# Two transformer layers on one core: a reordered routing chain, A.V in 32-column quarters in both layers, and identity products between the layers

## What is computed

```
x = x + tanh(g_xattn[0]) * L0_xattn(layernorm(x), ctx, ctx, mask)      # masked
x = x + tanh(g_ffn[0])   * L0_ffn(layernorm(x))                        # top-1 of 8 experts, 128 -> 512 -> 128, gelu
x = x + tanh(g_xattn[1]) * L1_xattn(layernorm(x), ctx, ctx)            # no mask
x = x + tanh(g_ffn[1])   * L1_ffn(layernorm(x))                        # top-2 of 16 experts, 8 slots each and batch
```

## Time and profile before

| | us |
|---|---|
| median of 3 runs | 534.26 (531.89 to 535.05) |
| the profiled execution's own time | 535.57 |
| its span, first to last instruction | 533.60 |
| layer 0 attention alone (TensorE all but uninterrupted) | about 17 to 184 |
| first experts | about 186 to 281 |
| layer 1 attention | about 289 to 440 |
| second experts, with the end of layer 1 | about 437 to 533 |

### The profile page before, as it was taken

One profiled execution on the slowest core, in us unless ns is written; L12 is line 12 of the kernel. 1 busy time (PEld: TensorE's weight loads), 2 busy tenths in 40 slices (PEclk: granted clock), 3 DMA queues, 4 the chain that ended last, 5 costly groups with the idle time before them and its releaser, 6 DMA issues.

```text
span 533.6 us, 19576 instructions
## 1 busy us (share of the span) xinstructions
PE 452.7 (85%) x7243; PEld 337.8 (63%) x7243; DVE 365.5 (68%) x977; ACT 322.0 (60%) x764; POOL 273.5 (51%) x325
## 2 busy tenths in 40 slices
PE   2789999998988896999985789988898777778887
PEld 1456776776776695999982466665565556444454
DVE  5678777978686857355542779889998786553455
ACT  2355565565765684677744566767667556775553
POOL 2522533556553347888886535353535316533455
PEclk9999999999999989799996799999999997899999
DMA  7114343232101134665445010110031000000112
GB/s 200 49 53 140 80 117 110 72 106 75 43 12 52 30 80 119 80 97 77 49 38 149 1 44 5 42 32 24 3 92 31 16 2 3 1 1 12 34 46 71
DMA packets 50620, 30.53 MB, mean 57 GB/s; under 512 B 12384, under 2 KB 46944, under 8 KB 50528
## 3 DMA queue, kind: packets, MB, share of 16 engines
q1 hardware_dynamic: 37072, 18.54, 12.9%
q0 software_dynamic: 6640, 4.67, 6.6%
q10 hardware_dynamic: 6816, 6.07, 4.0%
HBM read 19.41 MB, written 9.85 MB: 55 GB/s over the span
## 4 chain that ended last, share of the span: by engine, by line
PE 54%; DVE 14%; issue 13%; POOL 8%; ACT 6%; DMA 3%; ACTq 1%; DVEq 1%; SPq 0%; POOLq 0%
PE T_ps L861 8%; PE A_ps L876 7%; PE S_ps L850 7%; POOL x_mid L1140 6%; DVE maxes L603 5%; PE S_ps L844 3%; PE m_H_ps L1427 3%; PE Q_ps L831 2%; PE f_H_ps L1192 2%; PE m_T_ps L1467 2%; PE Q_ps L752 2%; PE m_X_ps L1454 2%; PE m_X_ps L1410 2%; PE X_ps L893 2%; PE Q_ps L763 2%
## 5 line engine op out<-in xcount | busy, mean ns | idle before, releaser
L603 DVE TENSOR_REDUCE maxes<-S_ps 128x8 f32<-128x512 f32 x128 | 87.6, 684 | 45.7 <-PE S_ps L850 45.6
L430 POOL TENSOR_TENSOR k_blk<-kT,col_a 128x512 f32<-128x512 f32 x64 | 67.7, 1068 | 86.2 <-ACT kT L491 59.7
L533 ACT ACTIVATE probT<-T_ps 128x512 f32<-128x512 f32 x128 | 76.0, 594 | 43.3 <-PE T_ps L861 42.8
L611 DVE TENSOR_TENSOR prob<-S_ps,maxes 128x512 f32<-128x512 f32 x128 | 88.5, 692 | 4.4
L861 PE MATMUL T_ps<-col_a,prob 128*128 128x128 f32 x512 | 83.2, 286 | 9.8 <-DVE prob L611 6.8
L861 PEld LDWEIGHTS T_ps<-col_a,prob 128*128 128x128 f32 x512 | 56.8, 143 | 47.1 <-issue 34.7
L1140 POOL DMA_INDIRECT x_mid<-f_out,f_rows x39 | 60.9, 1561 | 12.1 <-issue 10.7
L876 PEld LDWEIGHTS A_ps<-v_blk,probT 128*32 128x32 f32 (+1 forms) x3072 | 53.0, 119 | 10.6 <-issue 10.4
L876 PE MATMUL A_ps<-v_blk,probT 128*32 128x18 f32 (+1 forms) x3072 | 59.3, 195 | 0.0
L850 PE MATMUL S_ps<-k_blk,qT 32*64 32x256 f32 x1024 | 46.2, 415 | 5.4 <-DVE prob L611 2.9
L1005 DVE TENSOR_TENSOR f_hid<-f_H_ps,f_b 128x512 f32<-128x512 f32 x39 | 27.0, 692 | 33.3 <-PE f_Y_ps L1206 28.5
(11 more groups left out here) (198 smaller groups left out, 876.3 us busy)
## 6 DMA issues: line engine op xcount, KB each, us to landing
f_w<-in_W ACTq DMA_DIRECT2D x16, 256.0 KB, 2.8
ctxT<-in_ctxT SPq DMA_DIRECT2D x12, 256.0 KB, 3.1
f_rows<-sorted_rows SPq DMA_DIRECT2D x39, 64.5 KB, 2.0
out<-m_final SPq DMA_DIRECT2D x32, 64.0 KB, 1.5
x_all<-in_x SPq DMA_DIRECT2D x6, 256.0 KB, 5.0
x_mid<-x_all SPq DMA_DIRECT2D x6, 256.0 KB, 3.1
x_all<-x_mid SPq DMA_DIRECT2D x6, 256.0 KB, 3.7
ctxT<-in_ctxT SPq DMA_DIRECT2D x8, 128.0 KB, 2.6
```

The source lines that it names most:

```text
L430: nc.gpsimd.tensor_tensor(k_blk[:, t % 2, :, :, :], kT[:, g.at(R), t - g.first, :].rearrange("p (b k) -> p b k", b=2).unsqueeze(2).to_broa ...
L533: nc.scalar.activation(probT[:, t % 2, 4 * h:4 * h + 4, :], T_ps[:, :, :], ACT.Exp, scale=SCALE).then_inc(probT_ready, 1)
L603: nc.vector.tensor_reduce(maxes[:, t % 2, h, :, :], half_of(h), X, ALU.max).then_inc(max_ready, 1)
L611: nc.vector.tensor_tensor(prob[:, t % 2, heads, :].rearrange("p (r e) k -> p r e k", r=2), half_of(h), maxes[:, t % 2, h, :, :].unsqueeze( ...
```

## The change

1. **Ranks first.** `rank`/`rank_slots` move in TensorE's list from behind the last `logit` to directly behind the second half of `turn_probs`, ahead of `attend`; `keep_ranks` moves in ScalarE's list from behind `q_out` to directly behind the second `exp`. The times `when` stay.
2. **Single scatters.** In layer 0 the scatters of the groups 0 to 4 are laid one a step, where they were two a step.
3. **Quarters in layer 0 too.** `attend` and `logit` take 32-column parts in both layers.
4. **Identity products.** Matmuls of the identity with itself, whose results nobody reads and which wait for nothing. Five of 512 columns (`stream`) go into `tensor_ahead`, one behind each of its three `project_k` and two `project_v`, and three more (`STREAMED`) behind the last. Three (`awake`) go into layer 1's first steps, into T_ps: 256 columns behind the first `turn_x` (time 28.05), 256 behind the first `project_q` (30.01), 512 ahead of the first `turn_probs` (31).

```diff
--- before.py
+++ after.py
@@ -100,6 +100,7 @@
 EXPERTS_AT = MOVES_AT + NT // 8
 RAISE_AT = EXPERTS_AT + 5
 SINGLY = 7
+STREAMED = 3
 F1_PARTS = 4
 F1_FROM = NT + 19
 ONE_BY_ONE = GROUPS[SINGLY].first
@@ -476,7 +477,7 @@
             blocks = gpsimd_steps(pool)
             steps = [(blocks, tiles if masked else tiles[2:], shift(-2)), (norm, groups, head(-10)), (r_norm, groups, settled(3, 6, short, later))]
             if masked:
-                steps += [(scatter, tiles, lambda t: settled(8 if GROUP_OF[t].own < 7 else 7, 13, short, later)(GROUP_OF[t]) + (t - GROUP_OF[t].first) // 2)]
+                steps += [(scatter, tiles, lambda t: settled(8 if GROUP_OF[t].own < 7 else 7, 13, short, later)(GROUP_OF[t]) + (t - GROUP_OF[t].first) // (1 if GROUP_OF[t].own < LAST_GROUPS else 2))]
             else:
                 steps += [(gaps, groups, settled(7, 11, short, later))]
             steps += [(add_bias, groups, head(-4))]
@@ -587,8 +588,8 @@
                                          accum_out=r["total"][:, t:t + 1]).then_inc(raised_done, 1)
 
             k_out, v_out = scalar_steps(act)
-            steps = [(exp(1), tiles, shift(0)), (keep_logits, groups, settled(6, 9, short, later)), (avT_out, groups, tail(2)), (q_out, groups, head(-2)),
-                     (keep_ranks, groups, settled(7 if masked else 8, 12, short, later)), (v_out, late_units, unit_head(-1)), (k_out, late, head(-3)),
+            steps = [(exp(1), tiles, shift(0)), (keep_ranks, groups, settled(7 if masked else 8, 12, short, later)), (keep_logits, groups, settled(6, 9, short, later)), (avT_out, groups, tail(2)), (q_out, groups, head(-2)),
+                     (v_out, late_units, unit_head(-1)), (k_out, late, head(-3)),
                      (exp(0), tiles, shift(-1)), (r_xnT_out, groups, settled(5, 8, short, later)), (xnT_out, groups, turn_x_at), (normed, tiles, normed_at), (r_normed, units, lambda u: settled(4, 7, short, later)(u.group))]
             if not masked:
                 steps += [(raise_, groups[:SINGLY], tail(12)), (raise_last, [None], lambda _: RAISE_AT)]
@@ -766,9 +767,18 @@
 
             return project_k, project_v
 
+        def stream_into(bank, n):
+            eye = w["ident"][:, :]
+            nc.tensor.matmul(bank[:, 0:n, :], eye, eye.unsqueeze(1).to_broadcast([P, n, P]), start=True, stop=True)
+
         def tensor_ahead(pe):
             project_k, project_v = tensor_steps(pe, x_banks["q"])
-            return [(project_k, early, k_ahead), (project_v, early_units, v_ahead)]
+
+            def stream(_):
+                stream_into(S_ps[1][:, 0, :].rearrange("p (u k) -> p u k", k=P), Q)
+
+            return [(project_k, early, k_ahead), (stream, early, k_ahead), (project_v, early_units, v_ahead), (stream, early_units, v_ahead),
+                    (stream, range(STREAMED), lambda n: 2 * NT)]
 
         def tensor(pe):
             ident = w["ident"]
@@ -797,7 +807,7 @@
             def logit(g):
                 pe.wait_ge(r_xnT_ready, g.i + 1)
                 router_bank(g).take(logits_read, g.i + 1)
-                part = P if masked else QUARTER
+                part = QUARTER
                 for u in range(g.n):
                     for c in range(P // part):
                         rows = slice(c * part, (c + 1) * part)
@@ -869,7 +879,7 @@
                 pe.wait_ge(v_ready, u.i + 1)
                 wait(pe, divided, u.i)
                 pe.wait_ge(probT_ready, 2 * t + 2)
-                part = S if masked else QUARTER
+                part = QUARTER
                 for j in range(HP):
                     for c in range(P // part):
                         queries = slice(c * part, (c + 1) * part)
@@ -894,10 +904,13 @@
                 last.then_inc(y_made, 1)
 
             score_ahead = (score, tiles, score_at)
-            steps = [score_ahead, (turn_probs(1), tiles, shift(0)), (attend, tiles, shift(1)), (logit, groups[:7], settled(6, 9, short, later)),
+            awake = [] if masked else [(lambda n: stream_into(T_ps, n), [Q // 2], lambda _, when=when: when) for when in (NT - 3.95, NT - 1.99)]
+            awake += [] if masked else [(lambda n: stream_into(T_ps, n), [Q], lambda _: NT - 1)]
+            steps = [score_ahead] + awake + [(turn_probs(1), tiles, shift(0)),
+                     (rank if masked else rank_slots, groups, settled(7 if masked else 8, 12, short, later)), (attend, tiles, shift(1)), (logit, groups[:7], settled(6, 9, short, later)),
                      (turn_av, groups, tail(2)), (project_q, groups, head(-2)), (output, groups, tail(3)),
                      (logit, groups[7:], settled(6, 9, short, later)),
-                     (rank if masked else rank_slots, groups, settled(7 if masked else 8, 12, short, later)), (project_v, late_units, unit_head(-1)), (project_k, late, head(-3)),
+                     (project_v, late_units, unit_head(-1)), (project_k, late, head(-3)),
                      (turn_probs(0), tiles, shift(-1)), (turn_r, groups, settled(5, 8, short, later)), (turn_x, groups, turn_x_at)]
             run(hook["first_tensor"](pe) + steps + hook["tensor"](pe))
```

## The result

The kernel after takes 530.01 us (median of 9 runs, 528.1 to 534.7), the kernel before 534.26 (531.89 to 537.29); beside each other on one chip the ratio is 0.9908, 95% interval 0.9881 to 0.9934. The direction was forecast, the size was not: 9.9 us were expected, 4.3 to 5 came. The profiled execution took 529.13 (span 527.0), that of before 535.57: 6.4 apart.

The account below looks back on a forecast made before the run. TensorE was taken to bound layer 0, VectorE's need near. Terms 6.9 + 0.9 + 0.4 + 0.5 + 1.2 + 0.7 = 10.6, less 0.7 for new waits, give 9.9 us: from 534.26 to 524.3, range 520.5 to 528.5.

Parts of the forecast that it names:

- the loop's minimum: Layer 0: scores wait for the previous tile's subtractions, so no interval between tiles' first maxima falls much below 4.27 us.
- Rival A: VectorE or the new rank waits take most of the gain; layer 0 gives 3 us, total 530.5; chance 0.18.
- Rival B: All room in the intervals is used: 14.8 us in layer 0, 17.8 in all, total 516.5; chance 0.11.
- Rival C: TensorE's clock falls inside layer 0 because A.V is shorter; at eight tiles 15 us, total 539; chance 0.05.
- 1.2 together: Layer 1: bank waits removed by ranks first, in intervals with room 0.77, 0.65 and 0.26, give 1.2 us.
- 0.7 of it goes: Second experts: ScalarE's 1.02 us wait before keeping ranks, ahead of a normalization the experts' moves need, shrinks by 0.7 us.
- waits for the one-hot: Both layers: rank moved ahead waits for `choose` without A.V as cover; cost 0 to 5.7 us, taken as 0.7.
- Scatters, put at 0: Layer 0: single scatters only spread 16 scatters of about 1.0 us; gain 0, at most 1 either way.
- the term of layer 0: Savings summed interval by interval over layer 0, each capped by TensorE's room there: 6.9 us, ends 3 to 14.8.
- The handoff and the drain: Layer 0's end to the first up-product gains 0.9 us; one logit group in the first experts gains 0.4.
- Between the layers: Identity products keep TensorE's clock up; nothing before layer 1's first maximum, 0.5 us from the scores and products behind.
- Rival D: Identity products get in the way, the clock falls at 284 anyway; 6.4 us gained, total 527.9; chance 0.10.

Follow-up runs that it names:

- the first two sets: Kernel before with one part of the change each; then the whole, quarters again, and the whole less ranks or less identity products; ratios to before 0.9863 to 0.9998.
- only_ranks: Kernel before with only rank and keep_ranks moved ahead; ratio 0.9987 (0.9955 to 1.002).
- only_scatters: Kernel before with only single scatters in groups 0 to 4 of layer 0; ratio 0.9991 (0.9965 to 1.0016).
- row_reduced: Kernel after without VectorE's cast of the row numbers, the sum before it writing the integers itself; ratios to the kernel before 0.9933 and 0.9934.

## Why the prediction was wrong

**What held.** TensorE bounds layer 0, and quarters are the change: 187 ns for 212, the loop's minimum still 4.27, the stretch of the experts unchanged. Of the intervals, 2, 7, 10, 18, 22, 23 and 28 gave 0.26, 0.38, 0.38, 0.30, 1.16, 0.42 and 0.98, where 0.37, 0.37, 0.37, 0.30, 1.28, 0.37 and 0.91 stood; 24 and 27 gave nothing, as said. Rival A had the time nearly right (530.5) and in part for the right reason: the ranks of layer 1 give nothing; but VectorE's own need didn't cap layer 0 at 3. Rival B fell: layer 0 gave 5.8, not 14.8. Rival C was right that the clock falls inside layer 0, and wrong in the size: it stayed at 1.00 in the profiled execution, but fell in all seven other traces of the first two sets whose kernels change layer 0, for up to 1.9 us an interval, in one to three intervals, where C needed six to eight tiles. C's reason, the shorter A.V, is not shown: only_ranks and only_scatters leave A.V as it was and have a fall too. That the kernel after was profiled in an execution without a fall is luck.

**The step that failed: the ranks.** "1.2 together" for layer 1 and "0.7 of it goes" for the second experts. The prediction did price waits for the one-hot, at 0.7 of a possible 5.7, on the ground that they fall where TensorE idles for VectorE. It did not set them against the removed waits one by one. Side by side they are 5.10 and 5.56 us. From tile 37 to 58, where the 1.2 stood, the kernel takes 93.3 us with the edit and 93.4 without, and the ratio of the whole without it, 0.9909, can't be told from 0.9900. In layer 0 the ranks gave some 1.0 us in one pair of traces, half of it by where a held operation falls. In 14 and 22 the room is shared: ranks alone shorten them to 4.59 and 4.50, quarters alone to 4.71 and 4.31, both to 4.63 and 4.39. At the second experts nothing was seen to come back either: the rank that ScalarE kept after 1.02 us of waiting is now kept at once,

```profile
436.76 0.28 ACT L572 COPY rank_now<-Q_ps 128x128 f32<-128x128 f32 x1
```

and the stretch behind tile 58 is 1.0 us longer all the same, at a lower clock (0.88 for 0.92), so the 0.7 was not seen and is not disproved. The two terms are 1.9 us of the 9.9.

**Intervals that lengthened.** 11, 14 and 17 gave 0.58, 0.81 and -0.38 for 0.80, 1.17 and 0.72; 26 gave -0.67 for 0.19, and 3, to which nothing was assigned, gave -0.76. 3 and 26 are the held operations. The intervals that the prediction named gave 4.2 of their 6.9 us. Others, put at 0, gave 1.6: 15, 19, 21 and 25 came out 1.15, 0.38, 0.48 and 0.54 shorter, 3 and 29 0.76 and 0.21 longer. In 15, 19, 21 and 25 VectorE had no wait for scores in the row that ends the interval, so its filled time was read as its own need; in 15 and 19 that filled time held operations of `choose` that took 1.02, 0.97 and 0.94 us and could shorten. In 17 TensorE stood in the middle of the logits, now 32 short products where there were eight, with no wait that the profile shows. The logits in quarters alone lengthened it as well, to 5.90 and 5.91 us, and A.V alone shortened it to 4.93, so the stop comes with the quarters of the logits:

```profile
101.90 0.42 PE L814 MATMUL X_ps<-col_b,r_xnT 128*32 128x8 f32 x29
...
103.55 0.23 PE L814 MATMUL X_ps<-col_b,r_xnT 128*32 128x8 f32 x3 [1.22 <-issue]
```

**Scatters, put at 0.** From tile 1 to 20 the kernel before takes 95.4 us, scatters alone 93.9, quarters alone 94.0, the whole 92.3. So the trace of the kernel after holds some 1.5 us that the prediction had put down to nothing. Most of it comes from interval 15: before, two operations of `choose` took 1.02 and 0.97 beside two `k_blk` in a row (0.17 to 0.19 each elsewhere), with single scatters they lie apart and take 0.17 and 0.18. (Behind tile 20 single scatters shift time: alone they make 25 shorter by 0.53 us and 26 longer by 0.54.) Without this the term of layer 0, 6.9, would have come out near 4.3. In the times the scatters alone are not to be told from 0.

**The handoff and the drain**, 0.9 and 0.4, gave 0.5 and -0.1. **Between the layers** the products did hold the clock up to tile 32, and 0.5 was to come from the scores behind. There it fell after all, in a wait for VectorE:

```profile
289.93 0.66 PE L871 MATMUL T_ps<-col_a,prob 128*128 128x128 f32 x4 [2.50 <-DVE prob L612]
291.34 1.16 PE L860 MATMUL S_ps<-k_blk,qT 32*64 32x256 f32 x16 [0.76 <-DVE prob L612]
292.43 1.11 PE L871 MATMUL T_ps<-col_a,prob 128*128 128x128 f32 x4
```

The scores take 1.16 as in the earlier trace rows, 2.87 us behind the first maximum like there, though the fall lasts 3.4 us instead of 17.1: 0.1 of 0.5 came. Rival D was half right: not the products in the way, but the clock.

**The base.** The forecast was set from one profiled execution to the median of three runs. Later sets give 535.5 to 536.1 for the kernel before, so 534.26 was low by 1 to 2 us, and the ratio 0.9908 is 4.9.

**The account.** The stages of the trace add up to 6.5, 3.4 under the forecast: 1.7 behind tile 58, 1.3 in handoff, drain and between the layers, and 0.4 in layer 0 (1.1 less the 0.7 set off for waits). The 1.16 from tile 37 to 58 came out as forecast, but not from ranks. Between the 6.5 of the trace and the 4.9 of the times lies what differs from one execution to the next: the kernel's second profile gained 4.4 us in layer 0 instead of 5.8, for the two intervals with the clock down, and took 83.2 us for 82.5 behind tile 58.

## What to carry to other kernels

Moving a step ahead of what covered its input exchanges waits; list the removed and the new wait of every instance before giving it a gain. When intervals of a pipelined loop are summed, savings of two edits in one interval share its room, and each shift in time re-deals which short VectorE operations land beside a GpSimdE operation that reads. An identity product to hold the clock is paid for where TensorE has no real wait. And one trace is one execution: repeat the profile before reading a stage to a tenth of a microsecond, and look whether the clock fell in it.

## What was not expected of the hardware

Short VectorE operations of 0.15 to 0.19 us took up to 1.66 us beside GpSimdE, the longest (the cast) over a scatter and a `k_blk` in a row, and operations that read PSUM were never held. A scatter did not hold everything that a `k_blk` holds: in only_scatters `r_same`, with two inputs in SBUF, took 0.17 us at 96.76, with a scatter from 96.65 to 97.65. Writing integers from the sum instead of by a cast removed both the 0.17 us and the hold. TensorE's clock fell in layer 0 in one profile of the kernel after and not in the other, and at the start of layer 0 products took the times of the lower level for some 4 us longer in some kernels than in others, while the granted clock read 1.00. Late in layer 1 TensorE was busy 59.5 to 69.0 us with the same work. And two chips ran every kernel 20 us slower, with stops of 1.2 us inside A.V that carry no releaser; of the 25 us that the trace of row_reduced is longer than that of the kernel after, 11 lie in layer 0 and 13 between tiles 31 and 32. What these stops are was not tried.
